# Running sums for two neighbouring tokens at a time, reciprocal sums spread through DRAM, experts nine ticks later

## What is computed

```
x = x + attention16(xn) * silu(shared_and_routed_experts(xn))
x = x + linear_attention(xn) * silu(windowed_block(xn))

attention16: 16 heads of 64, causal softmax over 256 tokens
  attn = softmax(logits);  out = attn @ v
linear_attention: 16 heads of 8, q and k through elu + 1
  kv_cum = cumsum(k[..., :, None] * v[..., None, :], axis=2)
  k_cum  = cumsum(k, axis=2)
  out    = (q . kv_cum) / (q . k_cum + 1e-6)
windowed_block: two inner layers; each has local attention
  (8 heads of 64, window 64), then a layer norm and a gated block
```

## Time and profile before

| what | value |
| --- | --- |
| three runs | 2137.24, 2137.53, 2141.17 us, median 2137.53 |
| profiled execution | 2137.58 us, span of its instructions 2135.8 us |
| mean granted TensorE clock | 0.932 of full speed |
| DMA | 53.49 MB, mean 25 GB/s over the span |
| chain that ended last | PE 58%, DVE 12%, issue 11%, ACT 9%, POOL 9%, DMA 1% |

### The profile page before, as it was taken

One profiled execution on the slowest core, in us unless ns is written; L12 is line 12 of the kernel. 1 busy time (PEld: TensorE's weight loads), 2 busy tenths in 40 slices (PEclk: granted clock), 3 DMA queues, 4 the chain that ended last, 5 costly groups with the idle time before them and its releaser, 6 DMA issues.

```text
span 2135.8 us, 38268 instructions
## 1 busy us (share of the span) xinstructions
PE 1833.9 (86%) x12692; PEld 1166.5 (55%) x12692; DVE 1247.2 (58%) x4147; ACT 1207.0 (57%) x3559; POOL 754.3 (35%) x849
## 2 busy tenths in 40 slices
PE   6679989997999889997999889997999887787876
PEld 4358754663565455654565456654465455464554
DVE  4434446546755556646655556646756557767663
ACT  2444547655656665556656655656666555654643
POOL 2633226313622254213622244313622244525310
PEclk9789999999999999998999989999999998888978
DMA  8146500000000000000000000000000000000000
GB/s 236 41 159 209 178 16 6 6 1 1 6 2 16 1 1 6 16 1 1 6 2 16 1 1 6 17 1 1 6 1 11 1 6 1 1 6 1 1 2 10
DMA packets 49725, 53.49 MB, mean 25 GB/s; under 512 B 6386, under 2 KB 42236, under 8 KB 49532
## 3 DMA queue, kind: packets, MB, share of 16 engines
q0 software_dynamic: 7808, 27.79, 4.0%
q1 hardware_dynamic: 41724, 23.26, 3.8%
HBM read 41.60 MB, written 9.44 MB: 24 GB/s over the span
## 4 chain that ended last, share of the span: by engine, by line
PE 58%; DVE 12%; issue 11%; ACT 9%; POOL 9%; DMA 1%; SPq 0%; DVEq 0%; ACTq 0%; POOLq 0%; another core or an unknown queue 0%
PE ps L647 6%; PE ps L585 5%; PE ps L605 4%; PE ps L544 4%; PE ps L721 3%; PE ps L564 3%; PE ps L629 3%; PE ps L730 3%; PE ps L619 2%; PE ps L776 2%; POOL xn L305 2%; PE ps L767 2%; PE ps L769 2%; ACT p L865 2%; ACT p L864 2%
## 5 line engine op out<-in xcount | busy, mean ns | idle before, releaser
L1331 POOL COPY rdx<-rden 128x256 f32<-128x256 f32 x256 | 99.5, 418 | 612.6 <-DVE rden L1048 580.2
L1031 DVE CUSTOM_DVE_ANT_0 p<-ps,mask 128x128 f32<-128x128 f32 (+1 forms) x512 | 152.3, 353 | 265.6 <-PE ps L577 229.4
L1031 DVE CUSTOM_DVE_ANT_0 p<-ps,mask,nrq 128x128 f32<-128x128 f32 x512 | 149.0, 347 | 226.6 <-PE ps L573 225.9
L585 PE MATMUL ps<-ident,p 128*128 128x128 f32 x1280 | 224.1, 298 | 30.9 <-ACT p L865 28.1
L865 ACT ACTIVATE p<-p,nmax 128x128 f32<-128x128 f32 (+1 forms) x512 | 226.4, 442 | 0.0
L721 PE MATMUL ps<-wqkv,hT 128*128 128x512 f32 x384 | 196.2, 619 | 27.2 <-ACT big L944 25.6
L864 ACT ACTIVATE p<-p,nmax 128x128 f32<-128x128 f32 x512 | 200.3, 391 | 31.7 <-DVE nmax L1031 31.1
L879 ACT ACTIVATE pt<-ps 128x384 f32<-128x384 f32 (+1 forms) x256 | 111.6, 436 | 185.9 <-PE ps L585 182.4
L585 PEld LDWEIGHTS ps<-ident,p 128*128 128x128 f32 x1280 | 144.3, 148 | 113.7 <-issue 96.6
L1434 POOL TENSOR_TENSOR big<-big,rots 128x512 f32<-128x512 f32 x64 | 102.0, 1595 | 213.7 <-ACT big L944 213.7
L554 PE MATMUL ps<-ident,big 128*128 128x128 f32 x512 | 88.6, 312 | 91.1 <-DVE big L1226 43.2
(11 more groups left out here) (249 smaller groups left out, 4179.6 us busy)
## 6 DMA issues: line engine op xcount, KB each, us to landing
slots_in<-xn SPq DMA_DIRECT2D x1, 2560.0 KB, 13.9
v<-slots_in SPq DMA_DIRECT2D x20, 128.0 KB
slots_out<-v SPq DMA_DIRECT2D x20, 128.0 KB
big<-in_x SPq DMA_DIRECT2D x4, 512.0 KB, 6.1
x<-in_x SPq DMA_DIRECT2D x8, 256.0 KB, 3.3
out_x<-x SPq DMA_DIRECT2D x8, 256.0 KB, 2.3
wqkv<-in_wqkv SPq DMA_DIRECT2D x2, 768.0 KB
xn<-in_x SPq DMA_DIRECT2D x6, 256.0 KB, 3.3
```

The costliest lines, as they stand in the source:

```text
L585: last = nc.tensor.transpose(bank[:, j * P:(j + 1) * P], c.p[:, u % 4, j * P:(j + 1) * P], c.ident[:, :])
L1031: last = V.tensor_tensor_reduce(out=c.p[:, u % 4, a:b], in0=bank[:, a:b], in1=mask, scale=scale, scalar=3e38, op0=ALU.add, op1=ALU.min, ac ...
```

## The change

Three things change.

1. *Reciprocal sums spread through DRAM.* `merge`, `expand` and `rdx` go. PE transposes the 128x8 sums once, at the end of the second head's transposes of step s = 1 (8 partitions x 128). ACT copies that to `rdT`. DVE's `inverse` takes the reciprocal in place, now behind `scaled` of the pair before. SP's new `spread` stores the 4 KB to DRAM, waits for it, and loads each head's 512 values to 64 partitions of `rT`, of which there are now two, with two broadcast DMAs of 128 KB each. `scaled` waits for them.
2. *Running sums of two neighbouring tokens.* The tokens of a sequence are laid so that its tile pair holds even and odd tokens: partition i has tokens 2i and 2i+1. The input of `lin` is read with that stride, and the output of the linear attention is put back in order when it is evacuated (`oT`). POOL adds the even to the odd tile (1152 columns), PE makes one pass with a strictly triangular matrix for 4 heads at a time (288 columns), ACT copies it; POOL adds the even tile for the even token and the sum of both for the odd one, and then multiplies each by its q; DVE sums both. Eight passes a block stand where there were 18 (12 parts, 6 of them in two passes).
3. *The start.* Scatters stand in every second tick, 0 to 14. `e_at` goes from 8 to 17, the pauses from ticks 16 to 21 to ticks 16 to 36, and seven empty ticks behind them go. The table has 331 ticks.

```diff
-LCHUNKS = [(0, 6), (6, 5), (11, 5)]
+LPARTS = 4
+LHP = LH // LPARTS
+LN = LHP * LD * LE
...
-        e_at = 8
+        e_at = 17
         start = e_at + SLOT_PAIRS + 6
-        self.fill(start - 2, range(16, 22))
-        self.ticks += [None] * 7
+        self.fill(start - 2, range(16, 37))
+        self.fill(7, ())
         self.fill(8, ())
...
-            self.put(j, "scatter", j)
+            self.put(2 * j, "scatter", j)
...
-            for n in range(3 * TILES):
-                self.put(l0 + 1 + n + (n >= 6), "cum", b, n // 3, n % 3)
-                self.put(l0 + 2 + n + (n >= 6), "sum", b, n // 3, n % 3)
+            for n in range(2 * LPARTS):
+                at = l0 + 1 + n + 4 * (n >= LPARTS)
+                self.put(at, "cum", b, n // LPARTS, n % LPARTS)
+                self.put(at + 1, "sum", b, n // LPARTS, n % LPARTS)
...
-    c.den = sb("den", [P, 2, 4, 2])
-    c.rden = sb("rden", [P, 8])
-    c.rdx = sb("rdx", [P, TOK])
-    c.rT = sb("rT", [P, TOK])
+    c.den = sb("den", [P, 2, 2, 2, 2])
+    c.rT = [sb(n, [P, TOK]) for n in ("rT0", "rT1")]
+    c.rdT = c.sh2[3 * 32:3 * 32 + 8, 2, :]
...
+            if st.s and h:
+                den = c.den[:, st.pair % 2, :, :, :].rearrange("p h s i -> p (h s i)")
+                last = nc.tensor.transpose(bank[0:8, SB:SB + P], den, c.ident[:, :])
             last.then_inc(c.pt_full, 1)
...
-    def merge(pair):
-        bank = mm_bank("m", pair)
-        pe.wait_ge(c.rdx_ready, pair + 1)
-        for t in range(TILES):
-            last = nc.tensor.transpose(bank[:, t * P:(t + 1) * P], c.rdx[:, t * P:(t + 1) * P], c.ident[:, :])
-        last.then_inc(c.mm_full, 1)
...
+        tokens = c.xT[:, :].rearrange("p (s q u) -> p s u q", s=2, u=2)[:, t // 2, t % 2, :]
+        MM(bank[:, 0:3 * P], tokens, flat(c.lw), start=True, stop=True).then_inc(c.mm_full, 1)
...
-    def cum(b, t, part):
-        h0, nh = LCHUNKS[part]
-        bank = mm_bank("cum", b, t, part, 0)
+    def cum(b, seq, part):
+        bank = mm_bank("cum", b, seq, part, 0)
         if part == 0:
-            pe.wait_ge(c.kv_ready, TILES * b + t + 1)
-        a, n = h0 * LD * LE, nh * LD * LE
-        last = MM(bank[:, 0:n], c.tri[:, 0, :], c.kv[b][:, t % 2, a:a + n], start=True, stop=t % 2 == 0)
-        if t % 2:
-            last = MM(bank[:, 0:n], c.tri[:, 1, :], c.kv[b][:, 0, a:a + n], start=False, stop=True)
-        last.then_inc(c.mm_full, 1)
+            pe.wait_ge(c.kv_ready, TILES * b + 2 * seq + 2)
+        strict = c.tri[:, :, :].rearrange("p a n -> p (a n)")[:, P - 1:2 * P - 1]
+        MM(bank[:, 0:LN], strict, c.kv[b][:, 1, part * LN:(part + 1) * LN], start=True, stop=True).then_inc(c.mm_full, 1)
...
-    def merge(pair):
-        if pair:
-            act.wait_ge(c.o_done, o.done("o", pair - 1))
-        evacuate(c.rT[:, :], "m", pair)
...
-        A(c.pt[:, u % 4, 0:end], c.pt_ps[pt.slot("t", st.n, 1)][:, 0:end], ACT.Copy).then_inc(c.pt_done_act, 1)
+        bank = c.pt_ps[pt.slot("t", st.n, 1)]
+        last = A(c.pt[:, u % 4, 0:end], bank[:, 0:end], ACT.Copy)
+        if st.s:
+            if st.pair:
+                act.wait_ge(c.rd_stored, 16 * st.pair)
+            last = A(c.rdT[:, :], bank[0:8, SB:SB + P], ACT.Copy)
+        last.then_inc(c.pt_done_act, 1)
...
+    def cum(b, seq, part):
+        u = (2 * b + seq) * LPARTS + part
+        bank = mm_bank("cum", b, seq, part, 0)
         if u >= 2:
-            act.wait_ge(c.sum_ready, u - 1)
-        A(c.pr[b][:, u % 2, 0:n], bank[:, 0:n], ACT.Copy).then_inc(c.mm_done, 1)
+            act.wait_ge(c.sum_ready, 2 * (u - 1))
...
     def inverse(st):
-        dve.wait_ge(c.exp_done, 2 * st.n + 2)
-        if st.pair:
-            dve.wait_ge(c.rdx_ready, st.pair)
-        V.reciprocal(c.rden[:, :], c.den[:, st.pair % 2, :, :].rearrange("p u i -> p (u i)")).then_inc(c.rden_ready, 1)
+        dve.wait_ge(c.pt_done_act, pt.done("t", st.n, 1))
+        V.reciprocal(c.rdT[:, :], c.rdT[:, :]).then_inc(c.rden_ready, 1)
 
     def scaled(st):
         dve.wait_ge(c.pv_done, st.n + 1)
-        dve.wait_ge(c.mm_done, mm.done("m", st.pair))
-        TT(c.attT[st.kind][:, st.i, :], c.o_ps[o.slot("o", st.pair)][:, :], c.rT[:, :], ALU.mult)\
+        dve.wait_ge(c.rT_loaded[st.pair % 2], 32 * (st.pair // 2 + 1))
+        TT(c.attT[st.kind][:, st.i, :], c.o_ps[o.slot("o", st.pair)][:, :], c.rT[st.pair % 2][:, :], ALU.mult)\
...
+    def total(b, seq, part):
+        u = (2 * b + seq) * LPARTS + part
+        for a in range(2):
+            dve.wait_ge(c.prod_ready, 2 * u + a + 1)
+            TR(c.nd[b][:, 2 * seq + a, part * LHP * LE:(part + 1) * LHP * LE].rearrange("p (h e) -> p h e", h=LHP),
+               c.pr[b][:, u % 2, a, :].rearrange("p (h d e) -> p h e d", h=LHP, d=LD), axis=AX.X, op=ALU.add)\
+                .then_inc(c.sum_ready, 1)
...
-            if plan.step(tick - 1).s == 1:
-                inverse(plan.step(tick - 1))
         if (st := plan.step(tick - 3)) and st.s == 1:
             scaled(st)
+        if (st := plan.step(tick - 1)) and st.s == 1:
+            inverse(st)
...
-    def expand(pair):
-        pool.wait_ge(c.rden_ready, pair + 1)
-        if pair:
-            pool.wait_ge(c.mm_full, mm.full("m", pair - 1))
-        rd = c.rden[:, :].rearrange("p (s h i) -> p s i h", s=2, h=2)
-        for sq in range(2):
-            out = c.rdx[:, sq * SEQ:(sq + 1) * SEQ].rearrange("p (i h d) -> p i h d", i=2, h=2)
-            last = G.tensor_copy(out, rd[:, sq, :, :].unsqueeze(3).to_broadcast([P, 2, 2, HD]))
-        last.then_inc(c.rdx_ready, 1)
...
+    def cum(b, seq, part):
+        u, t = (2 * b + seq) * LPARTS + part, 2 * seq
+        pool.wait_ge(c.kv_ready, TILES * b + t + 2)
+        pool.wait_ge(c.mm_done, mm.done("cum", b, seq, part, 0))
+        pool.wait_ge(c.phi_ready, TILES * b + t + 2)
+        even, odd = (c.pr[b][:, u % 2, a, :] for a in range(2))
+        at = slice(part * LN, (part + 1) * LN)
+        G.tensor_tensor(even, odd, c.kv[b][:, 0, at], ALU.add)
+        link(G.tensor_tensor(odd, odd, c.kv[b][:, 1, at], ALU.add))
+        for a, pr in enumerate((even, odd)):
+            pr = pr.rearrange("p (g e) -> p g e", e=LE)
+            qq = c.qkb[b][:, t + a, part * LHP * LD:(part + 1) * LHP * LD].unsqueeze(2).to_broadcast([P, LHP * LD, LE])
+            G.tensor_tensor(pr, pr, qq, ALU.mult).then_inc(c.prod_ready, 1)
...
+        last = G.tensor_tensor(c.kv[b][:, t % 2, :].rearrange("p (h d e) -> p h d e", h=LH, d=LD), kk, vv, ALU.mult)
+        if t % 2:
+            link(last)
+            last = G.tensor_tensor(c.kv[b][:, 1, :], c.kv[b][:, 1, :], c.kv[b][:, 0, :], ALU.add)
+        last.then_inc(c.kv_ready, 1)
...
+    def spread(st):
+        sp.wait_ge(c.rden_ready, st.pair + 1)
+        sp.dma_start(dram.rd[st.pair].rearrange("(u q) -> u q", q=P), c.rdT[:, :]).then_inc(c.rd_stored, 16)
+        sp.wait_ge(c.rd_stored, 16 * (st.pair + 1))
+        if st.pair >= 2:
+            sp.wait_ge(c.o_done, o.done("o", st.pair - 2))
+        for h in range(2):
+            f = HD * h
+            sp.dma_start(c.rT[st.pair % 2][f:f + HD, :], dram.rd[st.pair][h * TOK:(h + 1) * TOK].partition_broadcast(HD))\
+                .then_inc(c.rT_loaded[st.pair % 2], 16)
+
     stage = {"xs": load_slots, "ed": store_slots, "xload": xload, "xres": xres, "fin": store}
     for tick in range(plan.length):
+        if (st := plan.step(tick - 1)) and st.s:
+            spread(st)
...
+    dram.rd = nc.dram_tensor("spread", (BLOCKS * 2 * PAIRS * LAYERS, 2 * TOK), FP32).ap()
```

More of the change, by code:

```diff
@@ L386, in buffers @@
     c.kv = [a[:, 0:2 * LH * LD * LE].rearrange("p (t n) -> p t n", t=2) for a in homes]
-    c.pr = [a[:, 2304:3168].rearrange("p (a n) -> p a n", a=2) for a in homes]
-    c.nd = [tiles(a[:, 3168:3744]) for a in homes]
+    c.pr = [a[:, 2304:2304 + 4 * LN].rearrange("p (u a n) -> p u a n", u=2, a=2) for a in homes]
+    c.nd = [tiles(a[:, 2304 + 4 * LN:2880 + 4 * LN]) for a in homes]
     c.v1 = sb("v1", [P, 2, TILES, INNER1])
@@ L486, in count_units @@
                 whitened[seg[0] == "ln2n"] += 1
-        if (st := plan.step(tick - 2)) and st.s:
-            mm.add(("m", st.pair))
     return mm, s, pt, o
@@ L669, in route @@
         hot = flat(c.hot)
-        MM(bank[:, 0:256], c.tri[:, 0, :], hot, start=True, stop=True)
-        MM(bank[:, 256:512], c.tri[:, 1, :], hot, start=True, stop=True).then_inc(c.cum_full, 1)
+        MM(bank[:, 0:256], c.tri[:, 1, :], hot, start=True, stop=True)
+        MM(bank[:, 256:512], c.tri[:, 2, :], hot, start=True, stop=True).then_inc(c.cum_full, 1)
     def eT(i):
@@ L753, in shift @@
         out, xa = halves(out, 1), halves(xa, 1)
-        MM(out[:, 0, :, :], c.tri[:, 2, :], xa[:, 0, :, :], start=True, stop=True)
-        MM(out[:, 1, :, :], c.tri[:, 2, :], xa[:, 1, :, :], start=True, stop=False)
-        MM(out[:, 1, :, :], c.tri[:, 3, :], xa[:, 0, :, :], start=False, stop=True).then_inc(c.mm_full, 1)
```

(13 more changed lines are left out.)

41 lines of the change are left out of this document (12 added, 29 removed).

## The result

The changed kernel is slower. Its runs have a median of 2155.47 us (2150.75 to 2157.56, 4 runs) against 2137.39 for the kernel before; the ratio is 1.0072, 95% interval 1.0057 to 1.0088, which is 15 us at 2137.4. The forecast was 2060, its range ended at 2108. The profiled execution, with 2150.75 us, is the lowest of its runs; its span is 2149.0 us against 2135.8, so the two traces differ by 13.2 us.

What follows compares the result with a forecast made beforehand. PE, busy 86%, was taken to bound the kernel. Savings of 47, 70, 8 and 17 (142 us), less 64 for relief given back, reciprocals, the end and POOL, made 2137.6 - 78 = 2060 us; range 2000 to 2108.

Steps and rivals of the forecast that it cites:

- DVE's longer reciprocals: Reciprocals of 8x128 on DVE: 99 us more work, mostly beside other work; 7 us on the path, bounds 0 and 49.
- given back: PE relief lost again as waits or clock: +32 us in six regular blocks, +15 in the last part.
- the start: Program start: fewer PE waits, better clock and a filled hole, against expert ticks without attention at +13; sum -17 us.
- the two prices of its relief: On PE: one transpose of 0.12 us replaces four of 0.49 per pair; running-sum passes of 288 columns take 0.58 us.
- rival 3: POOL and DVE block each other: 160 more POOL instructions stall DVE 118 us, a quarter on the path; +30, 2090; chance 0.09.
- A: Reciprocal sums through DRAM: one PE transpose per pair instead of four, saving 47 us of PE; POOL's copies go too.
- the two gains of 6 us for the clock and for the hole: In the start: better clock after fewer waits, 6 us; PE's idle hole at 287.00 to 317.70 filled with attention, 6 us.
- rival 4: The trip through DRAM becomes the wait in dense pairs: +137 us, 2197; chance 0.05, of which 0.04 slower.
- break-even of 9 us: Trip length through DRAM from which it would set the pace: a dense pair's 10.6 us less 1.65 on DVE.
- the prediction's other estimate, 4.3: DRAM trip by the skill's fixed cost: two transfers of about 2.0 us plus 0.3 for 128 KB, 4.3 us.
- the prediction's own rule: Relief in the dense stretch, where PE alone sets the pace, is kept; elsewhere half of it comes back.
- the 8 us that were taken for ACT's `rT`: Of PE's 11.8 us of waits for ACT's evacuated rT, 8 us were to go, as ACT gets a small copy.

Runs made afterwards that it cites:

- A alone: Only the reciprocal sums spread through DRAM, put on the kernel before; 2134.90 us, ratio 1.0005.
- C alone: Only the new start (scatters, experts' tick, pauses), put on the kernel before; ratio 0.9982.
- the wait for the norm: Changed kernel with one added wait: POOL's k times v of a block's second sequence begins after DVE's layer norm of the block before; 2117.05 us, ratio 0.9907.
- B alone: Only the running sums of two neighbouring tokens, put on the kernel before; 2106.69 us, ratio 0.9878.

## Why the prediction was wrong

**The step that failed.** The sum put the blocking of DVE by POOL at nothing and kept it as a rival with a chance of 0.09; it cost 35 us. It put DVE's longer reciprocals at 7 us; a run that leaves out 71 of their 121.5 us is 33 us faster. It took too little as given back where PE is nearly always busy, and misread what runs there, which leaves a remainder of 23 us. And it took 17 us for the start, where 4 came. That is 35, 26, 23 and 13 us, 97 in all, of the 95 that lie between 2060 and 2155.

**What bounds the kernel.** PE at 86% was read rightly, and the two prices of its relief that a row can check came as worked out. One transpose for four: PE L589 takes 0.11 us from start to start (1090.23 to 1090.34), 0.12 were taken. A running-sum pass takes 0.58 us (1091.44 to 1092.02), as worked out. What failed is the step from there to the time.

**The blocking (rival 3).** The rule was named, with its row, and was given a chance of 0.09 and 30 us. The size was near, 35 us, but not the place: the term was laid on POOL's 256 shorter additions and products, a quarter of them on the path. The measured loss comes from three long instructions in each of five blocks that fall on one root. The prediction said of k times v only that POOL "has room"; it never asked where POOL's stream would stand once its copies, and so its waits for each pair, were gone. Busy time of 58.0 in 152.3 us says nothing on that, and three of a block's four k times v are not even in that stretch. The rival and the reciprocal were also taken as alternatives, each in a case of its own, when they add up.

**The reciprocals.** 99 us more on DVE were worked out, 97 measured. Of them 7 were put on the path. The run with a copy takes 71 us off DVE and is 33 us faster (0.9918 against 1.0072), nearly half; by that share, an estimate, the 97 cost 45. That is near the upper bound of 49 that was given, and far from the fourteenth that was taken.

**The start.** -17 was the sum, -4 the measurement alone and none within the change. The expert ticks without attention cost what was taken: in the changed kernel PE waits 1.03 us in each of them, some 15 us (13 taken). What failed is the gain. The waits for `rdx` did go with A, 10.5 us as taken, but PE then only comes to the slots sooner: with A alone it waits 29.3 us for them, and the start part takes 359.4 us against 359.1. In the changed kernel PE was to wait 4.3 us for the slots and waits

```profile
136.25 0.66 PE L674 MATMUL ps<-ident,v 128*128 128x128 f32 x2 [10.02 <-DMA v<-slots_in]
```

Nine ticks more lie ahead of it, but the pauses begin at tick 16, so they hold no more attention and PE stands idle again. With C alone the wait fell to 2.9 us, as was hoped, and the start part became only 0.3 us shorter; the two gains of 6 us for the clock and for the hole show nowhere in it.

**The trip (rival 4).** Hidden, as forecast, 2.5 us at the end against 3 to 4. Its break-even of 9 us was wrong, as above. The shortest trip of 4.68 us is nearer to the prediction's other estimate, 4.3, than to its 5.6; the section of the Trainium skill behind the 4.3 is on transfers that GpSimd issues, though, and these are issued by SP.

**What is given back.** +32 and +15 were taken (half of 11.6 us in six blocks is 35, not 32). The places were misread. The prediction has the running sums between 926.50 and 1078.80 and few other stages between 838.50 and 926.50. The trace of the kernel before has it the other way round: from 838.50 to 926.50 stand all 18 passes of the block, two instructions each,

```profile
L730 PE MATMUL ps<-big,tri x24: 466/468/807, 847.2 to 921.7; 128*128 128x360 f32 x16, 128*128 128x432 f32 x8
L732 PE MATMUL ps<-big,tri x12: 466/496/807, 859.8 to 922.3; 128*128 128x360 f32 x8, 128*128 128x432 f32 x4
```

and from 926.50 to 1078.80 none. So 8.7 us of the sums and seven merges, 11.3 of the block's 14.6 us, lay where PE is busy 97% of the time. By the prediction's own rule they would all be kept, and they are not. Cut at the same attention steps, that stretch went from 88.0 to 89.7 us, with the wait for the norm to 83.2, and with B alone to 84.4. It too has its wait for `h`: 2.0 us before, 10.6 after, and 4.3 with the wait for the norm. A faster PE reaches it earlier and waits longer, as the prediction said of the other stretch. So 97% of busy time in a stretch did not mean that the relief there comes through.

With neither the blocking nor the reciprocal the time is 2089 (0.9771); the prediction's sum without its 7 us for reciprocals, and with the start at -4, is 2066. The 23 us between are what is left over, and no run splits them: they may be relief given back beyond the 47 taken, or the 8 us that were taken for ACT's `rT`, or the copy, which still takes 202 ns more for each pair than the reciprocal of before, 26 us on DVE. B alone, without the blocking at its full length, gives 26 us for 70 of relief less 6 for POOL. From 2089 the two single gains of 33 and 35 lead to 2157, against 2155.47 measured; that they add up is shown, the 23 us are only a remainder. The clock stands at 0.914 with the wait for the norm and at 0.916 without reciprocals as well; whether it would have stayed at 0.932 with fewer waits was not tried.

## What to carry to other kernels

Before an engine's instructions are removed, ask which waits go with them: they may be what keeps the rest of its stream in place, and a stream that runs ahead can meet another engine's critical chain. Where VectorE has a chain of small instructions on the path, look at what GpSimd runs at that moment and at how long each of its instructions is; a wait that costs GpSimd nothing can be worth more than the work that was saved. Changes are to be measured together as well as alone: here -26, +1 and -4 us made +15. And before a stretch is named after its stages, ask the trace which lines run in it.

## What the runs showed of the hardware that was not expected

A VectorE instruction on 128x4 elements that takes 0.16 us took 2.46 us beside a GpSimd instruction; all 28 instructions of that shape that took over 0.3 us in the changed kernel's trace end 0.02 to 0.03 us after a GpSimd instruction. After cutting GpSimd's work into pieces of 0.65 us, eight VectorE instructions in a row took 0.61 or 0.62 us each, one for one piece, so the two engines took turns, and the four instructions behind them took 2.95 us instead of 1.12. The reciprocal of 8 partitions x 128 takes 949 ns and that of 128 x 8 takes 193: its time goes with the elements of a partition, some 6.3 ns each, at 8 partitions as at 128. A copy of 8 x 128 takes 395 ns. A dependent round trip of 4 KB out and 2 x 128 KB back through DRAM took 4.7 us at its shortest from reciprocal to scaling, and the store alone 1.2 us from its issue to that of the load that waits for it.
